# Two-layer attention and MoE kernel: constants filled on the chip by ScalarE, every second expert weight tile made by GpSimd, loops over the blocks written out

## What is computed

```
# layer 0: causal attention, 16 heads of 8, an extra key and value from cond, projection
k = concat([k_img, k_word]); v = concat([v_img, v_word])
scores = einsum('bhqd,bhkd->bhqk', q, k) / sqrt(8); causal mask; + mask
a = softmax(scores) @ v @ c_proj_w + c_proj_b
# then an MoE of 8 experts, top 2 of a @ expert_tokens.T, each 128 -> 512 -> 512 -> 128
w = mean(topk_idx == i)
outputs += (gelu(gelu(a @ W1[i] + b1) @ W2[i] + b2) @ W3[i] + b3) * w
x = x + outputs
# layer 1: x times a weight modulated by cond and normalised, then an MoE of 8 experts with
# a capacity of 320 slots, top 2, softmax of the two logits, each 128 -> 512 -> 128
x = x + L1_ffn(L1_cond(x, cond))
```

## Time and profile before

| | us |
|---|---|
| median of 3 runs | 462.86 (460.72 to 464.38) |
| the profiled execution, its time | 464.21 |
| its span in the trace | 462.4 |
| mean granted clock of TensorE | 0.828 of full |
| PE / DVE / ACT / POOL busy | 313.4 / 282.1 / 176.4 / 135.5 |

### The profile page before, as it was taken

The page is one execution under the profiler, slowest core; times in us unless marked ns, Lnnn a source line. Parts: engine busy times, 40 slices in busy tenths (PEclk is TensorE's granted clock), DMA queues, the critical chain, the costliest instruction groups (busy, mean ns, idle before and its releaser), DMA issues.

```text
span 462.4 us, 8035 instructions
## 1 busy us (share of the span) xinstructions
PE 313.4 (68%) x2480; PEld 189.5 (41%) x2495; DVE 282.1 (61%) x719; ACT 176.4 (38%) x405; POOL 135.5 (29%) x161
## 2 busy tenths in 40 slices
PE   4550447999987777446579797989894436577820
PEld 2440223444444322225256555645552423365620
DVE  4870463888887755356875656655666683474623
ACT  1240004666643477150243333333346310544612
POOL 8800300001110144508324302121213047106670
PEclk9855676999999777756699989999998577689985
DMA  7985991256432088311425400000000301212114
GB/s 264 291 212 146 233 251 29 50 130 127 118 74 53 15 232 265 100 41 47 119 83 180 130 21 24 23 28 17 23 13 12 98 29 51 69 30 62 38 43 139
DMA packets 24802, 45.21 MB, mean 98 GB/s; under 512 B 4098, under 2 KB 14930, under 8 KB 24644
## 3 DMA queue, kind: packets, MB, share of 16 engines
q0 software_dynamic: 7280, 22.24, 17.9%
q1 hardware_dynamic: 14464, 15.32, 13.5%
q10 hardware_dynamic: 3028, 7.26, 4.4%
HBM read 28.33 MB, written 16.38 MB: 97 GB/s over the span
## 4 chain that ended last, share of the span: by engine, by line
PE 42%; DVE 15%; issue 13%; DMA 10%; SPq 10%; another core or an unknown queue 5%; ACT 3%; POOL 2%; ACTq 0%; DVEq 0%; POOLq 0%
PE pair L1093 15%; PE bank L990 4%; SPq L463 3%; DMA k_rows<-part 3%; PE bank L1104 3%; PE bank L968 2%; PE bank L1115 2%; DMA w_ring<-in_L_ffn_W_dram 2%; PE pair L1081 2%; PE pair L948 2%; DMA qr<-mrow 2%; PE bank L982 2%; SPq L485 2%; DMA back<-y_rows 2%
## 5 line engine op out<-in xcount | busy, mean ns | idle before, releaser
L1093 PE MATMUL pair<-w_sb,h 128*128 x276 | 68.1, 400 | 16.5 <-issue 9.4
L1416 DVE TENSOR_REDUCE mA<-pair 128x2 f32<-128x256 f32 (+3 forms) x64 | 50.9, 820 | 36.9 <-PE pair L950 36.3
L645 POOL DMA_DIRECT2D w_ring<-in_L_ffn_W_dram x24 | 21.5, 897 | 140.8 <-DVE w_sb L1357 108.7
L796 ACT ACTIVATE h<-pair,cols 128x128 f32<-128x128 f32 x92 | 26.2, 368 | 92.2 <-PE pair L1081 70.9
L784 ACT ACTIVATE p_ring<-bank 128x512 f32<-128x512 f32 (+1 forms) x88 | 45.9, 562 | 34.5 <-PE bank L971 34.4
L948 PE MATMUL pair<-kr,qr 128*128 128x128 bf16 (+3 forms) x122 | 32.8, 323 | 25.5 <-DMA kr<-k_rows 21.0
L693 POOL DMA_INDIRECT y_rows<-y_sb,id_now x21 | 24.5, 1167 | 86.0 <-DVE y_sb L1561 81.5
L1093 PEld LDWEIGHTS pair<-w_sb,h 128*128 128x128 f16 x276 | 26.3, 102 | 49.6 <-issue 23.9
L660 POOL DMA_INDIRECT x_slots<-sent,slot x32 | 31.1, 971 | 40.1 <-DVE slot L1671 16.7
L968 PE MATMUL bank<-qr,kr 128*128 128x384 bf16 (+3 forms) x120 | 33.4, 322 | 5.8 <-ACT p_ring L784 5.6
L948 PEld LDWEIGHTS pair<-kr,qr 128*128 128x128 bf16 x128 | 13.2, 105 | 47.8 <-issue 31.3
(11 more groups left out here) (293 smaller groups left out, 639.3 us busy)
## 6 DMA issues: line engine op xcount, KB each, us to landing
w_ring<-in_L_ffn_W_dram POOLq DMA_DIRECT2D x24, 512.0 KB, 5.8
x_slots<-w_sb ACTq DMA_DIRECT2D x2, 2064.0 KB, 10.9
kr<-k_rows SPq DMA_DIRECT2D x8, 272.0 KB, 4.8
qr<-q_rows SPq DMA_DIRECT2D x8, 256.0 KB, 4.1
fc_sb<-in_L_ffn_c_fc_dram POOLq DMA_DIRECT2D x4, 512.0 KB
cp_sb<-in_L_ffn_c_proj_dram POOLq DMA_DIRECT2D x4, 512.0 KB
back<-y_rows SPq DMA_DIRECT2D x8, 256.0 KB, 3.2
k_rows<-part SPq DMA_DIRECT2D x12, 136.0 KB, 2.7
```

The costliest lines, as they stand in the source:

```text
L796: ins = act.activation(to[:, c * P:(c + 1) * P], got[:, c * P:(c + 1) * P], ACT.Gelu, bias=cols[:, bass.ds(e * HC + (bias_row + c), 1)], s ...
L1093: ins = mm(bank(3), h1[:, s, hq, k * P:(k + 1) * P], w2_sb[k][wq][:, bass.ds(e * HID, HID)], start=(k == 0 and n == 0), stop=(k == HC - 1 ...
L1416: dve.tensor_reduce(mA[:, b, t, g * G + 2 * hp:g * G + 2 * hp + 2], got[:, :, 0:(t + 1) * P], AX_X, ALU.max).then_inc(a_used, 1)
```

## The change

- **Rows of q and k.** A row of DRAM is 48 high instead of 64, in another order of parts (Q_PART, K_PART), without constants and mask. The weights of q and k are reordered by dim on ScalarE (wqk), and so are two bias rows (rows_own) and ukT, so that a part can be stored in DRAM without reordering. store_parts issues three transfers for each of q and k instead of six, each as soon as its part exists.
- **Constants.** ScalarE fills all of qr and kr with one activation each, with a bias that is one (twice in bf16) on three partitions and zero elsewhere (fill, made by GpSimd). The mask goes from mpart straight into the slots (load_mask): once for the first four groups, then with three transfers for each later load, and one for zeros over the old maxima.
- **Queues.** Seven small loads go from ScalarE's queue to SyncE's, the two clears of x0 from ScalarE's to GpSimd's, behind the first four weight tiles.
- **Weight tiles.** A tile of W1 or W2 is two experts and all 512 columns, in runs of 2 KB. Twelve of 24 tiles (1, 3, ..., 19, 22, 23) are POOL_LOW: ScalarE only scales them in place, GpSimd makes the high part (a copy) and the low part (a subtraction). VectorE keeps 12.
- **Loops.** All 23 blocks are written out on the four engines, with one table value loaded for each block.

The diff, cut:

```diff
@@ -27,14 +27,13 @@
-Q_PART = (0, 0, 1, 1, 0, 2)
-K_PART = (0, 1, 0, 1, 2, 0)
-PROD_ROWS = len(Q_PART) * HD
-MASK_ROW = PROD_ROWS
-MAX_ROW = MASK_ROW + 3
-ZERO_ROW = MAX_ROW + 3
-ROWS = 64
+Q_PART = (0, 0, 0, 1, 1, 2)
...
 EARLY = 2
 PREPARED = 5
-W3_POOL = 2
-ROW_B1, ROW_B2, ROW_FC, ROW_QKV, ROW_PROJ, ROW_UK, ROW_UV, ROW_ET, ROW_IMG = (
-    0, E * HC, 2 * E * HC, 3 * E * HC, 3 * E * HC + 3, 3 * E * HC + 4, 3 * E * HC + 5,
...
@@ -417,17 +414,26 @@
         def w_tile(n):
-            cols_of = lambda c: slice(c * P, (c + 1) * P)
-            by_expert = lambda t, at: t[:, :].rearrange("p (e n) -> p e n", e=E)[:, :, at]
+            k, two = divmod(n, HC)
+            pair_of = slice(2 * two, 2 * two + 2)
+            in_pair = lambda t: t[:, 2 * two * HID:(2 * two + 2) * HID]
             if n < HC * HC:
-                k, m = divmod(n, HC)
-                return W2[:, cols_of(k), cols_of(m)], [by_expert(t, cols_of(m)) for t in w2_sb[k]]
-            k = (n - HC * HC) % HC
+                return (W2[pair_of, k * P:(k + 1) * P, :].rearrange("e p n -> p e n"),
+                        [in_pair(t) for t in w2_sb[k]])
             if n < HC * HC + HC:
-                return W1[:, :, cols_of(k)], [by_expert(t, cols_of(0)) for t in w1_sb[k]]
-            return W3[:, cols_of(k), :], [by_expert(t, cols_of(0)) for t in w3_sb[k]]
+                return W1[pair_of].rearrange("e p n -> p e n"), [in_pair(t) for t in w1_all]
+            k = two
+            return W3[:, k * P:(k + 1) * P, :].rearrange("e p n -> p e n"), [t[:, :] for t in w3_sb[k]]
+        def low_made(eng, n):
+            on_pool = [t for t in POOL_LOW if t <= n]
+            if n in POOL_LOW:
+                eng.wait_ge(w_lo_pool, len(on_pool))
+            else:
+                eng.wait_ge(w_lo, n + 1 - len(on_pool))
         sparse = 9
         high_at = [14 + 7 * n if n < sparse else 73 + 2 * (n - sparse) for n in range(W_EARLY)]
...
             def store_parts(b):
                 for i in range(2):
                     n = 2 * b + i
+                    rows = (k_rows_d if i else q_rows_d)[b].rearrange("(c d) h t -> (d h) c t", d=HD)
+                    width = IMG + S if i else S
+                    def store(first, last, m, copies):
+                        src = part[:, n, m:m + last - first, 0:width] if copies == 1 else (
...
+                            part[:, n, m:m + 1, 0:width].broadcast_to([P, copies, width]))
+                        sp.dma_start(rows[:, first:last], src).then_inc(rows_out[n], 16)
+                    sp.wait_ge(hi_ready, n + 1)
+                    store(*((5, 6, 0, 1) if i else (0, 3, 0, 3)))
+                    sp.wait_ge(act_step, n + 1)
+                    store(*((3, 5, 0, 1) if i else (3, 5, 1, 2)))
                     sp.wait_ge(parts_ready, n + 1)
-                    rows, which = (k_rows_d[b], K_PART) if i else (q_rows_d[b], Q_PART)
-                    width = IMG + S if i else S
-                    for c, m in enumerate(which):
-                        sp.dma_start(rows[c * HD:(c + 1) * HD].rearrange("d h t -> h d t"),
-                                     part[:, n, m, 0:width]).then_inc(rows_out[n], 16)
-            def zero_rows_of(n, width):
-                return mrowzero[:, :, 0:width].broadcast_to([H, n, width])
-            sp.wait_ge(consts, 1)
-            for b in range(B):
-                sp.dma_start(q_rows_d[b][MASK_ROW:MAX_ROW].rearrange("r h t -> h r t"),
-                             mrowone[:, :, IMG:]).then_inc(krest_out[b], 16)
-                sp.dma_start(q_rows_d[b][MAX_ROW:ROWS].rearrange("r h t -> h r t"),
-                             zero_rows_of(ROWS - MAX_ROW, S)).then_inc(krest_out[b], 16)
-                sp.dma_start(k_rows_d[b][MAX_ROW:ZERO_ROW].rearrange("r h t -> h r t"),
-                             mrowone[:, :, :]).then_inc(krest_out[b], 16)
-                sp.dma_start(k_rows_d[b][ZERO_ROW:ROWS].rearrange("r h t -> h r t"),
-                             zero_rows_of(ROWS - ZERO_ROW, IMG + S)).then_inc(krest_out[b], 16)
-                sp.dma_start(k_rows_d[b][MASK_ROW:MAX_ROW, :, 0:IMG].rearrange("r h t -> h r t"),
...
-            sp.wait_ge(mask_ready, 1)
-            for b in range(B):
+                    store(*((0, 3, 0, 1) if i else (5, 6, 2, 1)))
+            def load_mask(b, first, last, signal):
...
-                    sp.dma_start(k_rows_d[b][MASK_ROW + m:MASK_ROW + m + 1, :, IMG:],
-                                 mpart[b:b + 1, m:m + 1, :].broadcast_to([1, H, S])
-                                 ).then_inc(krest_out[b], 16)
+                    sp.dma_start(kr[MASK_ROW + m:MASK_ROW + m + 1, first:last, :, IMG:].rearrange("p s j t -> p (s j) t"),
+                                 mpart[b:b + 1, m:m + 1, :].broadcast_to([1, (last - first) * G, S])
+                                 ).then_inc(signal, 16)
             def rows_stored(b):
-                sp.wait_ge(rows_out[2 * b], 16 * len(Q_PART))
-                sp.wait_ge(rows_out[2 * b + 1], 16 * len(K_PART))
-                sp.wait_ge(krest_out[b], 16 * 8)
+                sp.wait_ge(rows_out[2 * b], 48)
+                sp.wait_ge(rows_out[2 * b + 1], 48)
             def load_rows(n):
                 b, g = divmod(n, NG)
                 if n >= SLOTS:
                     sp.wait_ge(s_done, s_index(n - SLOTS + 1, 0))
...
+            sp.wait_ge(trimmed, 1)
+            sp.wait_ge(mask_ready, 1)
+            load_mask(0, 0, SLOTS, masked)
             rows_stored(0)
-            sp.wait_ge(padded, 1)
             load_rows(0)
...
                 sp.dma_start(xg_lead[:, i, :], x0_d[i * SLOTS0:i * SLOTS0 + P, :]).then_inc(lead_in, 16)
-            with sp.Fori(0, LOOPS) as j:
-                first = table(mybir.EngineType.SP, 1, UNROLL * j + LEAD, UNROLL)
-                for n in range(UNROLL):
-                    load_block(j, LEAD + n, first[n])
-            first = table(mybir.EngineType.SP, 1, REST, NB - REST)
-            for i in range(REST, NB):
-                load_block(0, i, first[i - REST])
+            for i in range(LEAD, NB):
+                load_block(i, *table(mybir.EngineType.SP, 1, i, 1))
             for s in range(2):
                 sp.wait_ge(y_out[s], 16 * ((NB - s + 1) // 2))
...
             step = stepper(pool, pool_step)
+            step(pool.memset(fill[:, :], 0.0))
+            step(pool.memset(fill[MASK_ROW:MASK_ROW + 3, 1:2], ONES2))
+            pool.memset(fill[MAX_ROW:MAX_ROW + 3, 2:3], ONES2).then_inc(fill_ready, 1)
+            pool.wait_ge(fill_ready, 1)
...
+            pool.wait_ge(filled, 2)
+            pool.memset(kr[MAX_ROW:MAX_ROW + 3, :, :, 1:IMG], 0.0).then_inc(trimmed, 1)
             def load_weights(n):
                 if n >= W_RING:
-                    pool.wait_ge(w_lo, n - W_RING + 1)
-                pool.dma_start(w_ring[n % W_RING][:, :, :], w_tile(n)[0].rearrange("e p n -> p e n")
+                    low_made(pool, n - W_RING)
+                source = w_tile(n)[0]
+                pool.dma_start(w_ring[n % W_RING][:, :].rearrange("p (e n) -> p e n", e=source.shape[1]), source
                                ).then_inc(w_in[n % W_RING], 16)
+            def low_part(n):
+                pool.wait_ge(w_hi, n + 1)
+                hi, lo = w_tile(n)[1]
...
+                step(pool.tensor_copy(hi, w_ring[n % W_RING][:, :]))
+                pool.tensor_tensor(lo, w_ring[n % W_RING][:, :], hi, ALU.subtract).then_inc(w_lo_pool, 1)
             pool.wait_ge(qk_in[1], 32)
             for n in range(W_RING):
                 load_weights(n)
+            x0_clear = x0_d.rearrange("(h p n w) c -> h p n (w c)", h=2, p=P, w=CLEAR_RUN)
+            run = CLEAR_RUN * (2 * D + 2)
+            for h in range(2):
+                pool.dma_start(x0_clear[h], zeros[:, 0:run].rearrange("p (o c) -> p o c", o=1).broadcast_to(
+                    [P, x0_clear.shape[2], run])).then_inc(zero0_out, 16)
             for n in range(W_TILES - W_RING):
+                if n in POOL_LOW:
...
-            act.dma_start(vb_bc[:, :], attn_b[2 * D:3 * D].partition_broadcast(P)).then_inc(misc_in, 16)
-            act.dma_start(lw_sb, l1w.rearrange("a o i c -> (a o) (i c)")).then_inc(cond_in, 16)
-            for b in range(B):
-                act.dma_start(cond_bc[:, b, :], cond[b].partition_broadcast(P)).then_inc(cond_in, 16)
-            act.dma_start(mask_sb[:, :], mask.rearrange("b i j s -> (b i j) s")).then_inc(mask_in, 16)
-            act.dma_start(proj_sb[:, :], proj_w).then_inc(misc_in, 16)
-            act.dma_start(gate_sb[:, :], gate_w).then_inc(misc_in, 16)
-            x0_clear = x0_d.rearrange("(h p n w) c -> h p n (w c)", h=2, p=P, w=CLEAR_RUN)
...
+            act.wait_ge(fill_ready, 1)
+            for t, col in ((qr, 1), (kr, 2)):
+                flat = t[:, :, :, :].rearrange("p s j t -> p (s j t)").bitcast(F32)
+                act.activation(flat, fill[:, 0:1].broadcast_to([P, flat.shape[1]]), ACT.Identity,
```

(74 more changed lines are left out.)

267 lines of the change are left out of this document (138 added, 129 removed).

## The result

The changed kernel takes 433.39 us (432.44 to 433.74) beside 463.62 us (460.72 to 467.16) for the kernel before: ratio 0.9342, 95% interval 0.9273 to 0.941, or 30.2 us less. Forecast were 25 less: 438, range 427 to 453. In the profiled executions the spans are 431.4 and 462.4 us, which is 31.0; the points on the way show where they come from.

What follows compares the result with a forecast made beforehand. TensorE was taken to bound the middle of attention, not its end; its start waited on SyncE's queue, and expert layers lost time at turn ends. -22 + 3 + 4 + 2 - 12 = -25: predicted 438 us, range 427 to 453.

Steps and rivals of the forecast that it cites:

- Term 1: Start of attention: constants and mask leave SyncE's queue, so the second scores start 22 us earlier; bounds 13 and 26.
- gives back about 5 us: VectorE's set-up: with GpSimd's memsets of qr and kr gone, the 6.02 us stall of kimg_bd's products goes, about 5 us.
- rival A: Start of attention: the clears take the constants' place and the first maxima land at 60; 447 us, chance 0.12.
- Term 2: Middle of attention: weight tiles on GpSimd hold up steps of the maxima, +3 us; bounds 0 and 10.
- VectorE's relief: Middle of attention: VectorE is rid of 12 us of tile work, worth nothing or 1 us.
- E: GpSimd holds up every VectorE instruction that meets it, reductions too, so the kernel gets slower: 474 us, chance 0.04.
- Term 3: Last two groups of attention: GpSimd's tiles slow the round of tile slots, +4 us; bounds 0 and +9.
- Term 4: Ahead of the routing table: tiles 22 and 23 take GpSimd 6.6 instead of 4.2 us, +2 us; bounds 0 and 3.
- Term 5: Expert layers: written-out loops remove 14 us of turn ends, less 0.1 us per table value: -12 us; bounds -8 and -14.
- the argument against the branch: Expert layers: a 2.39 us gap stands ahead of the first turn, where no branch back has been taken.
- Rival D: Written-out blocks: streaming more code adds two or three long unexplained waits; 450 to 460 us, chance 0.07.

Runs made afterwards that it cites:

- e10: e7 with ScalarE's fill of kr moved behind the first batch entry's parts and the clears of x0 issued once the first maxima landed: 421.7 us, ratio 0.907.
- e6: The changed kernel with as much memset work on GpSimd as before, at the same place, on tiles not yet used: 432.2 us, ratio 0.928.
- e8: e7 with the clears of x0 issued only when the first maxima have landed: 422.5 us, ratio 0.908.
- e2: The changed kernel with the low parts of tiles 1, 3, ..., 19 back on VectorE, GpSimd keeping 22 and 23: 430.9 us, ratio 0.921.
- e7: e2 with ScalarE again making the high parts of tiles 22 and 23, GpSimd only subtracting: 429.2 us, ratio 0.921.
- e1: The kernel before with only the block loops written out and one table value loaded per block: 452.5 us, ratio 0.966.
- e4: The kernel before with its hardware loops kept and the table values loaded mostly one at a time, not in groups: 454.9 us, ratio 0.979.
- e3: The changed kernel, still without loops, with table values loaded in groups on every engine as the loops had them: 438.4 us, ratio 0.934.
- a_again: The changed kernel run once more, unchanged: 435.2 us, ratio 0.929 to the kernel before.
- e5: The changed kernel with the clears of x0 issued only after the load of weight tile 4: 434.8 us, ratio 0.933.

## Why the prediction came out as it did

The forecast was 25 us less, and 31.0 came out between the two traces. By the points of the table the five terms add up to -28.7, and two stretches that have no term add -7.2 and +4.8. That these two nearly cancel is luck, and with it part of the nearness.

**Term 1, start of attention: -22 forecast, -21.2 measured.** Right, by terms that partly cancel. That the constants' way through SyncE's queue was the 16 us is borne out by its rows; no run puts the constants back to show it alone. q came 3.6 us later for 3, and e10 shows for what. The step that failed is "gives back about 5 us": the stall was costed at its old length in an order in which q had just been put 3 us later. Moved against the memsets it would have lasted 1.9 us (e6). One wait was overlooked. In the kernel before, the first row of maxima was ready at 61.8, but SyncE issued it only at 64.38, behind its wait for the rows of the second batch entry:

```profile
54.75 9.57 DMA k_rows<-part
64.38 0.71 SPq L507
```

These 2.5 us went too; in the changed kernel the issue begins at 45.72, where the row was forecast for 45. The landing of the maxima, 51.9 against 51 taken, holds; e8 shows that the clears, which rival A spoke of, cost 3 us of it and not 9.

**Term 2, tiles in the middle: +3 forecast, -0.5 measured (+0.7 in the second trace).** The mechanism, maxima held and reductions not, is in the rows. Its size was too large: a step of 0.17 us grew to 1.8, but the stretch as a whole kept its length. VectorE's relief, taken as nothing or 1 us, may have made some of it good; e2 gives only both together. E, the rival that ended slower, falls with the 47 reductions.

**Term 3, last two groups: +4 forecast, +6.6 measured.** Mis-sized, inside its bounds of 0 to 9. The ring of four slots bounds this stretch; ScalarE's waits are for loads. VectorE's own low parts stood in GpSimd's way as well (subtractions of up to 3.0 us there), which was the far bound, and against e2 the tiles cost 8.5 us, since e2, with the new shape and without them, is 1.9 us quicker than before.

**Term 4, ahead of the table: +2 forecast, +0.6 in the trace; 2.2 by e7 against e2.** About right.

**Term 5, loops: -12 forecast, -14.3 measured, -13.9 alone (e1).** The values turned out wholly hidden: TensorE's timeline has no idle time from 210 to 309 us, where I had taken 0.1 us for each of 18 values. All 14 us of the gross sum came back. But the argument against the branch, a gap ahead of the first turn, said only that loading costs; e4 and e3 put 5 to 6 us to what goes with writing out, 8 to 9 to the loading in groups.

**Not forecast: 7 us gained behind attention, 5 lost in the second FFN.** From tile 19 to the slots of the second batch entry the changed kernel needs 7.2 us less. Some 2.4 of these lie ahead of TensorE's last eight products with v, which start 17.5 us sooner (185.57 and 168.10) where tile 19 came 15.1 sooner: the tile's wait of 2.06 us for its load held ScalarE more than TensorE. From these products to the slots are the other 4.8 us. The first part of that way, up to the projection, in the kernel before, e1 and the changed kernel; the third number from the end is the granted clock, 0.50 being 1.2 GHz and 1.00 2.4 GHz, and what lies between a mixture of both over the stretch:

```profile
185.57:196.76 11.19, 5.17 (x28) 3.25 (x29) 3.85 (x13) 1.60 (x2) 6.19 (x7) 0.72 0.31 95
```
```profile
185.02:193.01 7.99, 5.02 (x28) 3.37 (x29) 3.77 (x13) 1.60 (x2) 6.16 (x7) 0.72 0.44 135
```
```profile
168.10:175.22 7.12, 3.93 (x29) 2.71 (x29) 3.77 (x13) 1.46 (x2) 6.12 (x6) 1.00 0.78 204
```

The clock is the smaller part. e1 has the same code up to there as the kernel before and the same mean clock, 0.72, and is 3.2 us quicker: that is most of the 3.7 us by which it reaches the slots sooner (203.44 and 207.18). The chain of the kernel before shows where its 3.2 us lie:

```profile
185.57 1.60 PE bank L990 x8
191.33 1.58 issue
194.04 1.08 PE pair L1022
```

The same three steps take 0.41, 0.46 and 0.21 us in e1. Nothing that is recorded was waited for there. What TensorE stood still for stays open, and so does whether it repeats, for there is one trace of each; in e7 and e8 the first of the three steps takes 1.53 us too. Against e1, the changed kernel's full clock gives 0.9 us in this part, and 0.7 more up to the slots.

The second FFN is 4.8 us longer. 40 us of it, from 36.7 us behind the first sum, in the kernel before, the changed one and e8:

```profile
400.00:440.00 40.00, 33.51 (x343) 24.90 (x342) 24.68 (x66) 22.66 (x43) 16.67 (x16) 0.93 0.17 46
```
```profile
364.00:404.00 40.00, 32.13 (x285) 23.71 (x285) 22.38 (x62) 18.64 (x34) 13.34 (x14) 0.79 0.18 47
```
```profile
361.00:401.00 40.00, 32.98 (x338) 24.77 (x338) 24.54 (x67) 22.40 (x43) 16.34 (x16) 0.93 0.17 47
```

TensorE is busy about as long, and gets 285 instead of 343 products done: here each product takes longer, and it is the clock. In the 36 us ahead, its clock was 0.69 in both, busy 18.22 us in the kernel before and 20.32 in the changed one. At 0.93 this stage lasts 99.1 to 99.6 us (before, e8, e10), at 0.84 to 0.86 101.2 to 101.7 (e3, e4), at 0.79 to 0.83 102.9 to 105.8 (the changed kernel, a_again, e1, e2, e5, e6, e7). The written-out loops alone don't decide it: e1, the kernel before with them, has 104.6 us, but e8 and e10 have them too. Which edit tips the clock, and why, stays open. It is also why e8 and e10 gain more than their starts explain.

Rival D (longer code costs waits) finds no support: the waits that no record explains were there before, of 7.40 and 8.96 us, and in e8 and e10, whose blocks are written out too, the stage is as short as in the kernel before. (The blocks were written out on four queues; the prediction says five.)

## What to carry to other kernels

When two edits touch the same stretch, cost the second one in the schedule that the first leaves: a stall between two engines is as long as their overlap, and the overlap moves. Load registers behind a long instruction of the same engine, one at a time; that alone gave two thirds of what writing out the loops gave, and keeps the loops. A large transfer that nobody waits for (here 4.2 MB of clears) delays a small one that is waited for by about 3 us, so it belongs in a stretch with open queues; follow such a gain to the end of the trace, for here it was gone 130 us later. Moving work to an idle engine pays only where its old engine was the bound: here it lengthened a ring's cycle and lost 4 us.

## What the runs showed of the hardware that was not expected

- TensorE's granted clock in one and the same stage differs between kernels that are alike there, 0.79 to 0.93 over 40 us: 5 us of 430, more than most of the edits tried here. The two traces of the changed kernel have 0.79 and 0.83.
- TensorE stood still three times, 3.2 us in all, in one of two kernels with the same code up to there and the same mean clock (0.72), with no record that says for what.
- A memset on GpSimd stops VectorE's small tensor_scalar until it ends (1.86 and 6.02 us for 0.36) and lets a tensor_tensor of two f32 inputs pass (0.68 us); a subtraction on GpSimd stops that too (1.80 us for 0.17), and 47 reductions from PSUM keep their length to 4 ns beside GpSimd's copies and subtractions.
- A value loaded to a register behind twelve issued matmuls costs TensorE nothing; seven ahead of one cost 1.7 to 2.1 us without a branch anywhere (e3), and 2.39 ahead of the first turn.
